# Four heads per transfer, and the last query group's steps in periods 1 to 7 of the causal attention

## The reference

```python
x = x + _L0_xattn_ref(_layernorm(x), ctx, ctx, ...)      # softmax(q k^T / sqrt(8)) v, all keys
x = x + _L0_ffn_ref(_layernorm(x), gate_w, expert_w)     # x + expert_w[argmax(x gate_w)] x, 8 experts
x = x + _L1_xattn_ref(_layernorm(x), ctx, ctx, ...)      # the same attention with a causal mask
x = x + _L1_ffn_ref(_layernorm(x), router_w, gate_proj, up_proj, down_proj)   # top 2 of 8 experts
```

## Time and profile before

| | us |
|---|---|
| median of 3 runs | 809.38 |
| lowest and highest | 806.36, 813.43 |
| the profiled execution | 803.4 |
| its span, first to last instruction | 801.7 |
| PE busy | 624.9 (78%) |
| DVE busy | 479.0 (60%) |
| ACT busy | 393.0 (49%) |
| POOL busy | 359.3 (45%) |

### The profile page before, as it was taken

How to read it: one execution, slowest core, us unless ns; L and a number is a source line. 1 busy time by engine, 2 the same in 40 slices (tenths; PEclk the granted TensorE clock), 3 DMA queues, 4 the chain that set the end, 5 groups by cost and what they waited for, 6 DMA issues and landing times.

```text
span 801.7 us, 22693 instructions
## 1 busy us (share of the span) xinstructions
PE 624.9 (78%) x8205; PEld 476.0 (59%) x8205; DVE 479.0 (60%) x1255; ACT 393.0 (49%) x901; POOL 359.3 (45%) x555
## 2 busy tenths in 40 slices
PE   1574549989999599999798888888740999999980
PEld 1353326757676354554466666666530999999980
DVE  1462356767773367666666788888635455555545
ACT  0684425766677224543355666666630344444430
POOL 5484351101010234444243467777875355655550
PEclk9697767999999599999689999999955899999995
DMA  3389841545400793688308354400011222222219
GB/s 79 123 239 190 213 147 28 107 83 102 89 3 2 117 254 151 190 257 276 155 3 210 81 95 104 103 24 29 26 44 54 57 59 72 62 64 68 59 35 316
DMA packets 59708, 87.56 MB, mean 109 GB/s; under 512 B 8904, under 2 KB 50128, under 8 KB 56528
## 3 DMA queue, kind: packets, MB, share of 16 engines
q1 hardware_dynamic: 51024, 75.03, 36.8%
q0 software_dynamic: 4352, 8.99, 3.6%
q10 hardware_dynamic: 4224, 2.10, 0.9%
HBM read 43.99 MB, written 41.96 MB: 107 GB/s over the span
## 4 chain that ended last, share of the span: by engine, by line
PE 35%; issue 17%; DVE 10%; ACT 2%; SPq 1%; DMA 1%; POOL 0%; ACTq 0%; POOLq 0%; DVEq 0%
PE bank L1556 12%; PE bank L1564 6%; PE bank L1404 5%; DVE nm L926 2%; PE bank L711 1%; DVE e0ch L1345 1%; PE bank L653 1%; PE bank L1214 1%; PE bank L1544 1%; PE bank L1385 1%; PE bank L1395 1%; PE bank L693 1%; DVE e_qln_stats L339 1%; PE bank L722 1%; PE bank L670 1%
## 5 line engine op out<-in xcount | busy, mean ns | idle before, releaser
L808 ACT ACTIVATE pr<-bank 128x512 f32<-128x512 f32 x256 | 147.2, 604 | 77.4 <-PE bank L696 76.1
L926 DVE TENSOR_REDUCE nm<-bank 128x8 f32<-128x1024 f32 x128 | 155.7, 1221 | 48.8 <-PE bank L670 48.0
L1556 PE MATMUL bank<-exxt,qq 128*128 128x128 f32 (+1 forms) x864 | 109.2, 277 | 0.9 <-ACT exxt L1594 0.7
L1556 PEld LDWEIGHTS bank<-exxt,qq 128*128 128x128 f32 (+1 forms) x864 | 101.2, 185 | 1.6 <-ACT exxt L1594 1.1
L1098 POOL TENSOR_SCALAR_AFFINE_SELECT pr<-pr 128x1024 f32<-128x1024 f32 x64 | 69.8, 1091 | 64.4 <-ACT pr L808 63.4
L711 PE MATMUL bank<-pr,values 128*9 128x128 f32 x2048 | 82.0, 278 | 4.8 <-ACT pr L808 1.7
L1530 POOL DMA_INDIRECT results<-exy,exre x72 | 71.0, 986 | 30.2 <-issue 30.0
L693 PE MATMUL bank<-qq,kk 48*128 48x128 bf16 x1024 | 75.7, 221 | 6.8 <-ACT pr L808 5.0
L696 PE MATMUL bank<-mt,pick 64*128 64x128 bf16 x1024 | 75.8, 221 | 1.4 <-issue 1.4
L1404 PE MATMUL bank<-e0ch,expert_w 128*128 128x512 f32 x128 | 70.7, 635 | 6.5 <-DVE e0ch L1345 6.5
L1631 DVE TENSOR_TENSOR exhi<-bank,exsi 128x384 f32<-128x384 f32 x72 | 40.1, 558 | 56.3 <-PE bank L1556 40.2
(11 more groups left out here) (209 smaller groups left out, 1162.9 us busy)
## 6 DMA issues: line engine op xcount, KB each, us to landing
sorted_in<-values SPq DMA_DIRECT2D x25, 715.0 KB, 6.7
k_parts<-pj_parts SPq DMA_DIRECT2D x16, 384.0 KB, 4.1
kk<-k_parts SPq DMA_DIRECT2D x32, 192.0 KB
qq<-q_parts SPq DMA_DIRECT2D x32, 192.0 KB
exx<-sorted_in SPq DMA_DIRECT2D x72, 65.0 KB
kk<-k_parts SPq DMA_DIRECT2D x32, 128.0 KB
qq<-q_parts SPq DMA_DIRECT2D x32, 128.0 KB
q_parts<-pj_parts SPq DMA_DIRECT2D x8, 384.0 KB, 3.9
```

What stands on the lines that cost most here:

```text
L808: act.activation(probs[c], st_bank[(n * NC + c) % ST][:], ACT.Exp, scale=scale).then_inc(exp_s, 1)
L926: dve.tensor_reduce(neg_max[n % 2][:, u * 2 * C4:(u + 1) * 2 * C4], score_banks(n, u).rearrange("q (h k) -> q h k", k=T), AX_X, ALU.max, n ...
L1556: mm = pe.matmul(to[q.p][0:fn, f * T:(f + 1) * T], own_w[q.p][:, w0 + f0:w0 + f0 + fn], x, start=True, stop=True)
```

## The change

Each of the six transfers of `load_side` becomes two, of four heads (4 KB for a partition) each, and `QK_IN` doubles. The steps of `LAST` move from periods -3 to 3 to periods 1 to 7; `row_rstd` of `LAST`, so far at the end of `experts0` on POOL, gets period 2. Their transposes back (`z_bank`) go to bank 4, as the others of `LAST` do. The first transposes of routed rows on that bank wait for `rest0` of all groups. The tiles of `experts0` now share their memory with the tiles of `run_experts` rather than with the routed rows, and so the wait of `apply` for the stores is dropped. DVE's wait for `biased` moves to the first addition into the last group's sequences, in period 31. The order of SP's program isn't changed otherwise.

```diff
-QK_IN = 16 * 2 * 2 * len(RUNS)
+QK_IN = 16 * 2 * 2 * 2 * len(RUNS)
...
-TURN_BACK, APPLY, TURN_QUERIES, QUERIES, REST, CUT = -AHEAD, -1, 0, 1, 2, 3
+TURN_BACK, POWER, APPLY, TURN_QUERIES, QUERIES, REST, CUT = 1, 2, 3, 4, 5, 6, 7
...
-                    eng.dma_start(tile[g % QK_BUFS][row:row + count * DH], by_half[s]).then_inc(signal, 16)
+                    for u in range(2):
+                        heads = slice(u * C4, (u + 1) * C4)
+                        eng.dma_start(tile[g % QK_BUFS][row:row + count * DH, heads], by_half[s][:, heads]).then_inc(signal, 16)
...
-                top1 = ahead_of_it()
+                top1, expert_own = ahead_of_it(own)
...
                     pe.wait_ge(xn_s, bt.start + min(bt.count, G * h + G))
+                    if bt.i == 0 and h == 0:
+                        pe.wait_ge(top1.rest0, NG)
...
-                        if bt.i == 0:
-                            for p in range(2):
-                                act.wait_ge(top1.q_out[p], STORED * (NG // 2))
...
-                    if causal and n == 3:
+                    if causal and n - 3 == B - G:
                         dve.wait_ge(top1.biased, NG)
...
+                    if causal and n == POWER:
+                        row_rstd(pool, LAST, top1.q_ln)
...
-                bank[0], bank[1], bank[2:4], bank[4], bank[7], lambda g: bank[6 if g.n < LAST.n else 4], lambda g: bank[5 if g.n < LAST.n else 4])
+                bank[0], bank[1], bank[2:4], bank[4], lambda g: bank[7 if g.n < LAST.n else 4], lambda g: bank[6 if g.n < LAST.n else 4], lambda g: bank[5 if g.n < LAST.n else 4])
...
                 body(LAST, last=True)
-                row_rstd(pool, LAST, q_ln)
...
-        def top1_stage():
+        def top1_stage(own):
             with ExitStack() as its:
-                return experts0(its)
+                stage = experts0(its)
+            return stage, expert_tiles(own)
```

More of the change, by code:

```diff
@@ L1164, in attention @@
                 stage.listed = listed_s
-                stage.clear_vector, stage.clear_gpsimd, stage.top1 = clear_vector, clear_gpsimd, top1
+                stage.clear_vector, stage.clear_gpsimd, stage.top1, stage.expert_own = clear_vector, clear_gpsimd, top1, expert_own
                 stage.rows_moved = [(moved[p], sum(SENT * bt.count for bt in BATCHES if bt.p == p)) for p in range(ROWS)]
@@ L1179, in experts0 @@
             two = lambda name, shape, dt=F32: [sb(f"e0{name}{p}", shape, dt, own) for p in range(2)]
-            ln, q_ln = Norm("e0_ln", own), Norm("e0_qln", own)
-            xn_t, q_t = (two(k, [128, G * D]) for k in ("xt", "qt"))
+            parts, q_t = (list(reversed([sb(f"e0{k}{p}", shape, dt, own) for p in (1, 0)])) for k, shape, dt in (
+                ("parts", [128, 3, GT], BF16), ("qt", [128, G * D], F32)))
+            rest, q_ln = sb("e0rest", [128, GT], to=own), Norm("e0_qln", own)
+            y_t = sb("e0y", [128, GT], to=own)
+            ln, xn_t = Norm("e0_ln", own), two("xt", [128, G * D])
             top, best = two("top", [128, G]), two("best", [128, G])
@@ L1184, in experts0 @@
             hot = two("hot", [128, G, E], BF16)
-            chosen, y_t = two("ch", [128, GT]), sb("e0y", [128, GT], to=own)
-            parts, rest = two("parts", [128, 3, GT], BF16), sb("e0rest", [128, GT], to=own)
+            chosen = two("ch", [128, GT])
             padding = values[0][:].rearrange("p b h w -> p (b h w)")[:, 0:PAD * ROW].rearrange("p (n d) -> p n d", d=ROW)
             t_bank, sc_bank, hot_bank, y_bank, z_bank, qt_bank, q_bank = (
-                bank[0], bank[1], bank[2:4], bank[4], bank[7], lambda g: bank[6 if g.n < LAST.n else 4], lambda g: bank[5 if g.n < LAST.n else 4])
+                bank[0], bank[1], bank[2:4], bank[4], lambda g: bank[7 if g.n < LAST.n else 4], lambda g: bank[6 if g.n < LAST.n else 4], lambda g: bank[5 if g.n < LAST.n else 4])
             def x_of(g):
@@ L1200, in turn_back @@
                 for t in range(G):
-                    mm = pe.transpose(z_bank[:, t * T:(t + 1) * T], y_t[:, t * T:(t + 1) * T], ident[:])
+                    mm = pe.transpose(z_bank(g)[:, t * T:(t + 1) * T], y_t[:, t * T:(t + 1) * T], ident[:])
                 mm.then_inc(z_ps, 1)
@@ L1245, in add @@
                 dve.wait_ge(sum_s, g.n + 1)
-                dve.tensor_tensor(x_flat(g), z_bank[:], x_flat(g), ALU.add).then_inc(z_s, 1)
+                dve.tensor_tensor(x_flat(g), z_bank(g)[:], x_flat(g), ALU.add).then_inc(z_s, 1)
             def query_stats(dve, g):
@@ L1475, in experts0, with expert_tiles @@
             stage.cut, stage.bias = cut, bias
-            stage.biased, stage.q_out = biased, q_out
+            stage.biased, stage.q_out, stage.q_ln, stage.rest0 = biased, q_out, q_ln, rest0
             return stage
+        def expert_tiles(mine):
+            two = lambda name, shape, dt=F32: [sb(f"ex{name}{p}", shape, dt, mine) for p in range(2)]
+            x_g, x_t, y_g = two("x", [128, G, ROW]), two("xt", [128, GT]), two("y", [128, D])
+            share, result, aside = two("sh", [128, G]), two("re", [128, G], I32), sb("exas", [128, G], to=mine)
+            act_cell = sb("exact", [128, 1], to=mine)
+            silu, hidden = two("si", [128, len(FCH) * T]), two("hi", [128, len(FCH) * T])
+            return x_g, x_t, y_g, share, result, aside, act_cell, silu, hidden
         def run_experts(routed, mine):
@@ L1485, in run_experts @@
             blank_s, own_s, down_ps, y_s = (s(k) for k in ("blank", "own", "down", "y"))
[L1486 to L1489, removed]
+            x_g, x_t, y_g, share, result, aside, act_cell, silu, hidden = mine
             WIDE = len(FCH) * T
-            silu, hidden = two("si", [128, WIDE]), two("hi", [128, WIDE])
             t_bank, gate_bank, up_bank, y_bank = bank[0], bank[1:3], bank[3:5], bank[6:8]
@@ L1737, in build @@
             top1 = causal.top1
-            experts = run_experts(causal, own)
+            experts = run_experts(causal, causal.expert_own)
             total = combine(out, experts)
```

## The result

The changed kernel takes 813.82 us in the median (810.93 to 818.49, 20 runs) against 807.75 us for the kernel before (802.26 to 814.15, 20 runs, in the same sessions). The ratio is 1.0087, with a 95% interval of 1.0064 to 1.0109: slower, clear of the scatter, by 6.1 us between the medians and some 7 us by the ratio. That is at the lower edge of the range of 813 to 831. The forecast had the sign, the place and the cause of the loss, but it said +12.9 us, about twice the loss that was measured. The profiled run of after took 811.11 us (span 809.4) against 803.4 (span 801.7), +7.7 us.

The account below looks back on a forecast made before the run. The prediction took PE to bound the steady causal attention, with the entry periods longer. A wait of +11.2, +2 half clock, +0.7 late code and -1 for the split gave +12.9 us, 822.3 us on the median, range 813 to 831.

Parts of the forecast that it names:

- What is taken away at the entry, and what comes in: Causal attention's entry and periods 1 to 7: -5.6 us for steps removed, their return added, -1.6 us together.
- +0.65, +0.66 and +1.10: Microseconds added by `query_apply` on ScalarE in period 3, `turn_queries`' transposes in period 4, and product `queries` in period 5.
- the +0.5: Causal attention, periods 4 to 6: 0.5 us added for all the moved copies on ScalarE and VectorE.
- The wait behind the moved `cut`: SP's queue holds group 3's rows behind the store awaiting `cut`; PE stands some 17 us, period 9 starts +11.2 us later.
- Behind the stall: After PE's wait before period 9: +2 us for half clock, +0.7 us for late code in periods 9 to 11.
- Four heads at a time: Halved loads: rate unchanged, late code of attention 0 may pass sooner, -1 us taken between 0 and -3.84.
- The projection: Loads there double to 24 issues, but SP is already held by a full DMA queue: 0 taken, +4.8 us upper end.
- The sum: Whole kernel: 11.2 + 2 + 0.7 - 1 = +12.9 us, 822.3 us on the median; chance 0.57.
- The wait is short: Group 3's load takes 10 us, full clock returns at once, attention 0 loses both stalls: +5.4 us, 815; chance 0.17.
- Halved transfers are fast: Loads take 5 us, shortening the period 9 wait, attention 0 and the projection: -11.6 us, 798; chance 0.08.
- SP's issues bind: Twelve more issues ahead of the projection's rows of x cost +4.8 us, longer half clock +3: 830 us; chance 0.15.
- Nothing waits at period 9: Group 3's rows arrive by 440.3, so PE has no wait there: -6.2 us, 803; chance 0.03.

Follow-up runs that it names:

- e2_move_only: The changed kernel with whole transfers of eight heads again, so only the steps of the last group are moved: 822.29 us, ratio 1.0177 to before.
- e1_split_only: The kernel before with only the halved transfers of four heads, the last group's steps where they were: 796.28 us, ratio 0.9867.
- e9_whole_spaced: The kernel before with whole transfers, each followed on SP by a tiny one into a spare tile, 24 issues a load: 797.34 us, ratio 0.9851.
- e6_quarter: The kernel before with transfers of two heads, 48 issues a load, the steps where they were: 844.18 us, ratio 1.0465.
- e3_load3_first: The changed kernel with SP issuing the query and key rows of group 3 ahead of the last store of query parts: 795.22 us, ratio 0.9853.
- e4_no_a0_loads: The kernel before without attention 0's loads of groups 3 to 7: 802.67 us, four runs in two pairs (794.79 and 796.41, 808.93 and 809.58).

## Why the prediction was half right

**What is taken away at the entry, and what comes in: right.** -5.6 and +1.1 up to period 3 make -4.5; e2_move_only, where only the move acts, has -4.8 in that column, and after -4.7. From P3 to P6 the forecast's +0.65, +0.66 and +1.10, with most of the +0.5, make some +2.7; it was +3.7. The difference is `query_apply`: +1.55 us instead of +0.65. I had put it between "it fits" and "none does"; it was all but the latter, because it stood ahead of a copy that PE needs at a fixed place in the period. The free time of ScalarE, added up over the period, said nothing on that.

**The wait behind the moved `cut`: right, term by term.** The store came 7.03 us into period 7 (forecast 7.04). From the store to the rows it was 21.0 us (19.8), and SP's 24 issues held it up (12.7 us to hand over, 7.9 before), within the 1.5 that the forecast allowed for them. PE stood 17.96 us ("some 17"). Counted from the first score block of the causal attention, period 7 began at 47.6 us, forecast 46.8.

**Behind the stall: sized too high.** +2 was forecast for half clock and +0.7 for late code. The clock had fallen to 0.50 at 440.7 us, while PE stood, and was back 3.2 us after the wait, and period 9 took 461.66 - 454.57 = 7.09 us against 6.37 before: +0.7. No stretch without a releaser came in periods 9 to 11. Together 2.0 us too much.

**Four heads at a time: the step that failed.** The forecast had the right effect in view ("smaller pieces may also let the late code of attention 0 pass sooner") and took -1 us of it, out of a bound of 0 to -3.84. The column of attention 0 became 5.0 us shorter, 4.0 more than taken and beyond the bound (4.4 us of it in the attention itself), since that bound counted only the two stretches of the earlier trace rows in one profiled run. By the medians the split is worth -8.5 us beside the move and -11.7 alone. Two things were wrong in the way it was sized. The bound came from a single execution, while such a stretch isn't the same from kernel to kernel: 2.15 us in before, 3.52 and 4.39 us in two kernels with the same transfers. And the gain was kept to attention 0. The causal attention has a stretch too; I took that away from period 6 only because its traffic moved, and added half of one again behind the stall. In e1_split_only 4.5 us come from there and 2.2 from the shorter half clock at the entry, for which the forecast had no term. The reason was off as well: the gain came without smaller pieces too (e9_whole_spaced), so it is more likely the slower pace of SP's issues that lets the code pass.

**The projection: right.** Taken at 0; DVE's waits for x were 29.9 us after and 31.0 before, and attention 0 started at 113.4 and 113.5. The twelve more issues are hidden there. e6_quarter shows where they no longer are.

**The sum.** On the profiled runs, +12.9 with 4.0 less for attention 0, 2.0 less behind the stall, 1.2 more for the rows and 0.8 more up to period 7 is +8.9; +7.7 was measured, and the difference is what the two last columns of the table differ by (337.8 against 336.7), where nothing was changed. On the medians, e2_move_only at 822.29 us lies on the forecast of 822.3, and that is luck: it leaves out the split, to which the forecast gave -1. Its profile has 22.2 us from the store to the rows, and the causal attention begins 4.0 us later than before, 1.7 of it by a later start of attention 0 and 2.3 by a longer one, with stretches of the kind that the split cures.

**The rivals.** "The wait is short" (815 us) came nearest in number, but not by its mechanism: it had the wait at 15 us and both stretches of attention 0 gone. The stretches did go; the wait was longer than forecast, not shorter. "Halved transfers are fast" was wrong on the rate (154 GB/s against 140) and on the projection. "SP's issues bind" needs 48 issues, not 24. "Nothing waits at period 9" was excluded rightly; e3_load3_first shows what it is worth.

## What to carry to other kernels

When a step that ends in a store is moved later, follow the queue behind that store first: here one wait in SP's order cost 18 us, and the moved steps themselves gave back about 1. And when a trace has idle stretches of an engine without a releaser while large loads are issued back to back, look whether code arrives shortly before PE goes on, and try issuing the same loads at half the pace; the price is the queue's issue time, so count what else that queue carries. Don't size such an effect by the stretches that one profile happens to show; run the cheap half of the change alone. The scatter of the runs didn't size it either: it was 12 us in before and 6 in e1_split_only, but 4.0 in e2_move_only, which has the stretches (6 runs), and 14.8 in e4_no_a0_loads, which has none in attention 0 (4 runs).

## What was not expected of the hardware

- Whole transfers of 8 KB a row, handed over at half the pace by tiny ones between them, made the kernel 10.6 us faster (807.92 to 797.34), although more was transferred.
- Where nothing holds it up, an issue on SP's queue takes 0.38 us for a whole transfer (2.25 us for six) and 0.39 for a halved one (4.66 us for 12); under the fills twelve took 8.03 us. 12, 24 and 48 issues for the same bytes gave 808, 796 and 844 us, so the best of the three lies in the middle, with the stretches on one side and the queue on the other.
- PE stood for up to 4.39 us with nothing that the program explains, and went on 1.3 to 1.8 us after a 16 KB transfer of code had arrived.
- After 18 us of idle PE the granted clock was 0.50 for another 3.2 us only, then 1.00; at the entry of the causal attention it was 0.50 for 17.1 us in the kernel before and for 6.8 us in e1_split_only, with the same work there.
